# Row maxima taken singly and in pairs, and five score banks at the end, in a fused attention and expert layer

## The reference, cut to what matters

```python
Q, K, V = (layernorm(x) @ W.T + b for W, b in ...)          # 16 heads of 16 features, 2 sequences
scores = einsum('bhqd,bhkd->bhqk', Q, K) / 4
A = softmax(scores, axis=-1)
A_stable = 0.6 * A + 0.4 * L                                # L: a band of width 7, equal for all heads
x = x + einsum('bhqk,bhkd->bhqd', A_stable, V) @ Wo.T + bo
x = x + moe(layernorm(x))                                   # top 2 of 4 experts
```

## Time and profile before

| | |
|---|---|
| time, median of three runs | 1935.2 us (1935.0 to 1937.52) |
| time of the profiled execution | 1934.62 us |
| its span, first to last instruction | 1932.8 us |
| TensorE, share of the span busy | 98% |
| VectorE | 84% |
| ScalarE | 67% |
| GpSimd | 19% |
| granted TensorE clock, mean | 0.995 of full speed |

### The profile page before, as it was taken

The page is one execution under the profiler, slowest core; times in us unless marked ns, Lnnn a source line. Parts: engine busy times, 40 slices in busy tenths (PEclk is TensorE's granted clock), DMA queues, the critical chain, the costliest instruction groups (busy, mean ns, idle before and its releaser), DMA issues. The chain is left out here.

```text
span 1932.8 us, 41897 instructions
## 1 busy us (share of the span) xinstructions
PE 1889.9 (98%) x16092; PEld 1116.2 (58%) x16092; DVE 1629.0 (84%) x3147; ACT 1299.1 (67%) x2390; POOL 372.0 (19%) x380
## 2 busy tenths in 40 slices
PE   7999999999999999999999999999998999999997
PEld 3554444444444444444444444444586899999997
DVE  6799999999999999999999999994277755555554
ACT  3348888888888888888888888888544422322232
POOL 1362110010101110101010101011045622223233
PEclk9999999999999999999999999999999999999999
DMA  7954456645564556455645454543246777878884
GB/s 258 260 111 90 89 113 111 107 90 112 109 109 90 112 106 112 89 114 101 113 92 114 100 111 95 104 100 82 91 139 209 286 226 221 257 253 256 288 255 113
DMA packets 132021, 279.65 MB, mean 145 GB/s; under 512 B 41696, under 2 KB 72416, under 8 KB 125152
## 3 DMA queue, kind: packets, MB, share of 16 engines
q1 hardware_dynamic: 118672, 259.17, 53.6%
q0 software_dynamic: 13152, 17.83, 4.7%
HBM read 215.93 MB, written 79.06 MB: 153 GB/s over the span
## 5 line engine op out<-in xcount | busy, mean ns | idle before, releaser
L677 DVE TENSOR_REDUCE part_max<-psum 128x1 f32<-128x512 f32 x2048 | 1232.8, 676 | 4.3 <-PE psum L782 3.0
L738 ACT ACTIVATE probs<-psum 128x512 f32<-128x512 f32 x2048 | 1064.4, 601 | 169.2 <-PE psum L791 162.8
L782 PE MATMUL psum<-max_k,max_q 48*128 48x512 f32 x2048 | 696.1, 459 | 0.1
L791 PE MATMUL psum<-score_q,score_k 50*128 50x512 f32 x2048 | 629.8, 428 | 0.8 <-issue 0.6
L803 PE MATMUL psum<-probs,v_ones 128*32 128x256 f32 x8192 | 601.6, 388 | 6.4 <-ACT heads_sb L744 6.3
L782 PEld LDWEIGHTS psum<-max_k,max_q 48*128 48x128 f32 x2048 | 316.6, 183 | 224.1 <-DVE part_max L677 205.3
L791 PEld LDWEIGHTS psum<-score_q,score_k 50*128 50x128 f32 x2048 | 320.2, 184 | 198.4 <-ACT probs L738 146.3
L803 PEld LDWEIGHTS psum<-probs,v_ones 128*32 128x32 f32 x8192 | 188.1, 108 | 257.6 <-issue 146.0
L1236 ACT ACTIVATE x_sb<-psum,x_sb 128x512 f32<-128x512 f32 (+1 forms) x160 | 101.7, 636 | 260.0 <-PE psum L1607 257.8
L1626 PE MATMUL psum<-w,h_hi 128*128 128x256 f32 x1120 | 208.5, 282 | 0.1
L1626 PEld LDWEIGHTS psum<-w,h_hi 128*128 128x128 f32 x1120 | 181.0, 188 | 10.8 <-DVE h_lo L1426 0.3
(11 more groups left out here) (177 smaller groups left out, 1242.5 us busy)
## 6 DMA issues: line engine op xcount, KB each, us to landing
w<-w_split SPq DMA_DIRECT2D x40, 2048.0 KB, 8.5
max_q<-qk_pieces SPq DMA_DIRECT2D x192, 128.0 KB, 6.9
score_k<-qk_pieces SPq DMA_DIRECT2D x192, 128.0 KB, 4.6
xs<-in_pads SPq DMA_DIRECT2D x33, 528.0 KB, 4.6
qk_pieces<-pieces SPq DMA_DIRECT2D x32, 512.0 KB, 4.7
w_split<-w_pair SPq DMA_DIRECT2D x32, 512.0 KB, 5.3
max_k<-qk_pieces SPq DMA_DIRECT2D x192, 64.0 KB, 7.1
score_q<-qk_pieces SPq DMA_DIRECT2D x192, 64.0 KB, 2.3
```

Of the source, the lines that this page charges most:

```text
L677: nc.vector.tensor_reduce(part_max[:, u, t, q:q + 1], ps_m[q // 2][:, 1 - q % 2, :], axis=AXIS.X, op=ALU.max).then_inc(m_read, 1)
L738: nc.scalar.activation(probs[:, kb % PROBS, chunk * BLOCK:(chunk + 1) * BLOCK], bank_of(k, kb, c), ACT.Exp, scale=float(HD) ** -0.5).then_ ...
L782: nc.tensor.matmul(ps_m[p][:, h, :], max_q[u][rows, t * P:(t + 1) * P], max_k[u][rows, p * BLOCK:(p + 1) * BLOCK], start=True, stop=True). ...
L791: nc.tensor.matmul(bank_of(k, kb, c), score_k[u][rows, kb * P:(kb + 1) * P], score_q[u][rows, part * BLOCK:(part + 1) * BLOCK], start=True ...
```

## The change

VectorE takes blocks 0 and 1 of a step one by one and blocks 2 and 3 in one instruction over both banks of `ps_m[1]` (1024 columns): three reduces a step in place of four, `READS = 3`, and blocks 2 and 3 of the next step both wait for the pair. TensorE's round is written in another order. The loop with maxima runs 246 rounds (`MIXED`) in place of 256. The last 20 key steps have a loop of their own: four scores, then both value parts. From unit 1972 on (`WIDE_FROM`) the scores go round five banks, the three of `ps_s` and the two of `ps_m[0]`; the first use of the added two waits for all maxima. In the last head the band product and `mix_heads(0)` use `ps_m[1]` for that reason.

```diff
+READS = 3
-def mix_heads(nc, dve, keep, i):
+def mix_heads(nc, dve, keep, i, at):
...
-                                       keep["psum"][:, 4 + m, :], ALU.mult, ALU.add).then_inc(keep["a_copied"][m], 1)
+                                       keep["psum"][:, at + m, :], ALU.mult, ALU.add).then_inc(keep["a_copied"][m], 1)
...
+    MIXED = -(-(NHEADS * ST - LOOK) // 2)
+    WIDE_FROM = 2 * CH * MIXED + CH
+    WIDE = RING + 2
+    wide = [ps_s[(WIDE_FROM + i) % RING] for i in range(RING)] + [ps_m[0][:, c, :] for c in range(2)]
     def bank_of(k, kb, c):
-        return ps_s[(k * UNITS + CH * kb + c) % RING]
+        unit = k * UNITS + CH * kb + c
+        return ps_s[unit % RING] if unit < WIDE_FROM else wide[(unit - WIDE_FROM) % WIDE]
...
         def maxima(g, t, u, between=None):
-            for q in range(4):
-                if q == 2 and between is not None:
-                    between()
+            for q in range(2):
                 dve.wait_ge(m_ready, 4 * g + q + 1)
-                nc.vector.tensor_reduce(part_max[:, u, t, q:q + 1], ps_m[q // 2][:, 1 - q % 2, :],
+                nc.vector.tensor_reduce(part_max[:, u, t, q:q + 1], ps_m[0][:, 1 - q, :],
                                         axis=AXIS.X, op=ALU.max).then_inc(m_read, 1)
+            if between is not None:
+                between()
+            dve.wait_ge(m_ready, 4 * g + 4)
+            nc.vector.tensor_reduce(part_max[:, u, t, 2:3], ps_m[1].rearrange("p b f -> p (b f)"),
+                                    axis=AXIS.X, op=ALU.max).then_inc(m_read, 1)
         def split_shift(m, u):
-            dve.wait_ge(m_read, 4 * ST * (m + 1))
+            dve.wait_ge(m_read, READS * ST * (m + 1))
...
-        mix_heads(nc, dve, keep, 0)
+        mix_heads(nc, dve, keep, 0, 6)
...
             if g > 0:
-                pe.wait_ge(m_read, 4 * g + q - 3)
+                pe.wait_ge(m_read, READS * (g - 1) + min(q + 1, READS))
...
         def scores(n, k, kb, c):
-            if not isinstance(n, int) or CH * kb + c >= RING or n > 0:
-                pe.wait_ge(exp_done, count_of(n, kb, c) - RING)
+            unit = count_of(n, kb, c) - 1
+            if WIDE_FROM + RING <= unit < WIDE_FROM + WIDE:
+                pe.wait_ge(m_read, READS * ST * NHEADS)
+            elif unit >= RING:
+                pe.wait_ge(exp_done, unit + 1 - (WIDE if unit >= WIDE_FROM + WIDE else RING))
...
-                local_values(nc, keep, psum[:, 4 + m, :], 0, m).then_inc(keep["a_ready"][m], 1)
+                local_values(nc, keep, ps_m[1][:, m, :], 0, m).then_inc(keep["a_ready"][m], 1)
```

More of the change, by code:

```diff
@@ L885, in fill @@
                 pe.wait_ge(keep["band_in"], 16)
-                pe.wait_ge(m_read, 4 * ST * NHEADS)
-                local_values(nc, keep, psum[:, 4 + m, :], 0, m).then_inc(keep["a_ready"][m], 1)
+                pe.wait_ge(m_read, READS * ST * NHEADS)
+                local_values(nc, keep, ps_m[1][:, m, :], 0, m).then_inc(keep["a_ready"][m], 1)
             if kb in FIRST_HEADS:
@@ L897, in _ @@
             score()
-        for _ in range(NHEADS * ST // 2):
+        for _ in range(MIXED):
             score()
+            maximum()
+            maximum()
+            score()
+            value()
+            score()
+            score()
+            maximum()
             maximum()
@@ L903, in _ @@
             value()
-            maximum()
-            maximum()
+            value()
             score()
[L907 to L911, removed]
             maximum()
@@ L915, in _ @@
             maximum()
-            score()
             maximum()
             value()
+        for _ in range(NHEADS * ST - 2 * MIXED):
+            for _ in range(CH):
+                score()
+            for _ in range(PARTS):
+                value()
 def route_and_experts(nc, ctx, dram, keep, block):
@@ L1462, in _ @@
         nc.vector.reciprocal(keep["inv_tok"][:], keep["sum_tok"][:]).then_inc(inv_ready, 1)
-        mix_heads(nc, dve, keep, 1)
+        mix_heads(nc, dve, keep, 1, 4)
         for i in range(BLOCKS):
@@ L1480, in _ @@
             if i + 2 < BLOCKS:
-                mix_heads(nc, dve, keep, i + 2)
+                mix_heads(nc, dve, keep, i + 2, 4)
         weigh(BLOCKS - 2)
@@ L1721, in program @@
                 keep["bias_v"] = head_sb("bias_v", [P, DIM])
-                for n, shape, dt in (("part_max", [P, 2, ST, 4], F32), ("neg_max", [P, ST], F32),
+                for n, shape, dt in (("part_max", [P, 2, ST, READS], F32), ("neg_max", [P, ST], F32),
                                      ("shift", [P, PIECES, ST], F32R), ("shift_tok", [P, PIECES * ST], F32)):
```

## The result

The changed kernel takes 1917.7 us (median of four runs, 1915.6 to 1922.6) against 1936.4 beside it: a ratio of 0.9906, interval 0.9890 to 0.9922. It is faster by 18.6 us where 33 were forecast. The profiled execution has a span of 1915.8 us against 1932.8.

The account below looks back on a forecast made before the run. VectorE was taken to bound the kernel. Pairs 33.7, less boundaries 7.5 and shift 1.0, plus the end 7.8, save 33.0 us: from 1934.6 profiled to 1902; range 1890 to 1916 (0.83), likeliest case 1896 to 1909.

Parts of the forecast that it names:

- What bounds the kernel: Stretch of 31 heads: VectorE bounds it at 38.93 us a head, with TensorE close behind.
- the pair's price: VectorE's 1024-column reduce: successor 1.13 us behind, saving 0.066 a step, 33.7 us over 511 steps.
- TensorE's pace: TensorE's rounds: least round stays 4.60 us against VectorE's 4.65 and small operations; thin margin, but it holds.
- The boundary: Between heads: VectorE stands still 0.3 to 0.4 us, net 0.17 to 0.27; 7.5 us over 30 boundaries.
- the fourth score: Round behind a boundary: it needs an exponential delayed by `copy_o`; M2 and M3 behind it miss their 2.99 deadline.
- The chain: TensorE's sequence in the new order: next M0 at 2.78, 0.21 us before its deadline, and waits again.
- The shift: DMA chain to a head's first score: enough slack ordinarily; two or three late heads, 1 us in all.
- The slack of the last wait: Head's first score waiting for the shift: slack 0.7 us in place of 1.4.
- The end: Last maximum to last copy: 44.7 us against 52.5, saving 7.8; ends 5.5 and 10.
- the shift's catch: In the end stretch: shift lands at 10.6 us, ScalarE has work until 11.2; one catch of 0.4.
- five rivals: No boundary loss 0.17, TensorE's pace 0.21, nothing from pairs 0.09, slower 0.06, fixed part saved whole 0.02.
- the one in which TensorE sets the pace: Rival, chance 0.21: neighbours in one array half cost more, round 4.80 us, time about 1910 to 1912.

Follow-up runs that it names:

- experiment 7: Changed kernel with TensorE's maxima of blocks 2 and 3 ahead of the two scores in every round: 1957.1 us (1.0101 of the kernel before).
- Experiments 5: Changed kernel with maxima of blocks 2 and 3 ahead of the two scores in every eighth round, behind head boundaries: 1917.5 us (0.9900).
- 6: On top of experiment 2, maxima of blocks 2 and 3 ahead of the two scores in every eighth round: 1908.5 us (0.9849).
- 8: On top of experiment 2, `copy_o` copies 32 of 512 columns, leaving out most of the attention's output: 1894.8 us (0.9784).
- experiment 2: Changed kernel; SP carries the shift before storing the finished head, GpSimd splits it before normalising that head: 1905.9 us (0.9834).

## Why the prediction was wrong

- **What bounds the kernel, the pair's price.** Right: 1.13, a step 2.327 by its starts, 33 us if nothing else.
- **TensorE's pace.** Right: no loss in ordinary rounds. That the margin is thin experiment 7 shows; its size doesn't follow from the 4.60 us a round of the prediction.
- **The boundary.** Size right: 0.43 a time in the median (0.41 in the head shown), against 0.3 to 0.4; net 0.3, 9 us for 7.5. Part of the mechanism wrong: it isn't the pair's place behind the fourth score. The chain put the next M0 at once on time, and left out what else waits for the copy. Experiments 5 and 6 against 8 show that the copy's length makes the loss and the order doesn't; that the scores behind wait on delayed exponentials too is my reading.
- **The shift.** The step that failed: "enough in an ordinary head. Two or three late heads pay some 0.5 more each: 1 us." It was eight heads, 12.1 us of lateness in place of 1.1, and another 1.8 us in the head where the clock fell; experiment 2 gives 12 of it back. The slack of the last wait (0.7 of 1.4) was worked out nearly right: 7.40 less 6.3 is 1.1. But I took the way to it as fixed ("keep their place in SP's queue"). Two things on it moved. The time from the inverse of the sums (key step 4) to `neg_max` (key step 10) shrank from 14.56 to 14.18 us, while the DMAs between take as long as ever, so that the store of the finished head now ends behind the transpose in 21 of heads 1 to 30, against 4 before. (Its end moved by 0.6 in the median; 0.38 of that is this stretch, and most of the rest a longer wait in SP's queue ahead of the store of the inverse.) And a leg that leaves late costs 1.2 to 1.8 more where it meets a fetch. Both show in the kernel before: late head 18 of the earlier trace rows isn't an accident with a rate of its own, but the case that comes when the store is late and a fetch is near. I read its size and not its cause.
- **The end.** Off by 2.5 us: 47.2 for 44.7, 5.3 saved for 7.8. ScalarE's idle time before exponentials was 6.6 us in place of 5.7: the shift's catch took 1.4 for 0.4, because the last head's leg too was slow (3.4). Its pace where it ran on was 0.48, as taken; that is luck, since the row it was taken from gives (3.05 - 0.6) / 5 = 0.49. And the sum left a term out: at each of nine stops ScalarE also loses the overlap with the row before, whose 0.59 to 0.82 us run out where the next one otherwise starts 0.48 behind; that is 1.7 us in all. The last wait took 1.25 where 1.5 were in the sum. In experiment 2 the same stretch took 49.4 us; there the granted clock was 0.50 from 1309 to 1315 us, around TensorE's wait for the last shift. The waits of the changed kernel at the shift and at one projection (TensorE, then ScalarE):

```profile
1321.28 0.50 PE L804 MATMUL psum<-score_q,score_k 50*128 50x512 f32 x2 [2.30 <-DMA score_q<-shift_dram]
```

```profile
1321.85 1.09 ACT L748 ACTIVATE probs<-psum 128x512 f32<-128x512 f32 x2 [1.41 <-PE psum L804]
...
1347.10 2.06 ACT L748 ACTIVATE probs<-psum 128x512 f32<-128x512 f32 x4 [0.66 <-PE psum L804]
```

With the shift's edit the changed kernel stands at 1905.9 us, 4 above the forecast of 1902; that is what the other terms were off by, less the earlier start. None of the five rivals is what happened: they move the pairs, the boundary or TensorE's pace, and none the shift. The measured 1917.7 lies nearest to the one in which TensorE sets the pace (1910 to 1912), but its sign, heads of 38.4 us and more throughout, isn't there.

## What to carry to other kernels

When the bounding engine gets faster, go through every chain of DMAs that runs beside it from one of its instructions to another: the chain doesn't shrink, and its slack does, at each link. In an in-order DMA queue the urgent transfer belongs ahead of the one with time; here that cost nothing before the change and was worth 12 us behind it. A rare late case in the old trace is worth a look at what makes it late, not only at how late it is. When moving a late instruction's neighbours only moves the wait, the engine may be late as a whole: look for what took its time.

## What the runs showed of the hardware

- In 51 of 360 legs a transfer of 4 KB met a fetch of instructions on the same DMA engines: with one of 16384 bytes it landed 1.0 to 2.0 us later than the rest, with one of 8192 bytes alone 0.4 to 0.7. Nothing in the engines' rows shows it; only the instruction row of the DMA queues in a window of 2 us does.
- Behind a wait of TensorE for a late shift (1.27 us in head 28) the granted clock was 0.50, 1.2 GHz, where it had been 1.00, and the head took some 1.8 us more. Seven late heads with waits of 1.0 to 1.6 us show no fall in the same trace; what decides it no run here tells.
- VectorE's starts can be late by up to 0.08 us with no idle time in its rows, as neighbours overlap by that much. In experiment 7 26 of some 60 us lost were of this kind.
- A maximum over 1024 columns in two PSUM banks took 1.211 us, its successor came 1.13 behind: the second bank costs 0.533 us, where a maximum of its own costs 0.598.
